# A layer of attention in which odd key runs swap their high and low parts, and the low-part score products of a piece's two halves run in rows 0 to 63 and 64 to 127 of the array

## What is computed

```python
qkv = x @ Wqkv + bqkv
...
scores = jnp.einsum('hnd,hmd->hnm', qh, kh) * SCALE
scores = scores + graph_bias * adj_matrix[None, :, :]
scores = jnp.where(attn_mask[None, :, :] == 0, jnp.float32(-1000000000.0), scores)
attn = jax.nn.softmax(scores, axis=-1)
out = jnp.einsum('hnm,hmd->hnd', attn, vh)
...
x = _layernorm(x + _L0_gnn_ref(x, adj, adj, L0_gnn_Wqkv, L0_gnn_bqkv, L0_gnn_Wout, L0_gnn_bout, L0_gnn_graph_bias), axis=-1)
x = _layernorm(x + _L1_gnn_ref(x, adj, L1_gnn_W, L1_gnn_a), axis=-1)
x = _layernorm(x + _L2_gnn_ref(x, adj, L2_gnn_W, L2_gnn_b), axis=-1)
x = _layernorm(x + _L3_gnn_ref(x, adj, L3_gnn_W), axis=-1)
```

## Time and profile before

| | |
|---|---|
| median of 3 runs | 2980.61 us (2979.36 to 2982.26) |
| the profiled execution's own time | 2979.79 us |
| its span | 2978.0 us, granted clock 0.997 |
| TensorE matmuls busy | 2938.3 us, 99% of the span |
| VectorE, ScalarE busy | 2090.7 us (70%), 1893.6 us (64%) |
| attention in its steady state | about 160 to 1557 us of the span |

### The profile page before, as it was taken

How to read it: one execution, slowest core, us unless ns; L and a number is a source line. 1 busy time by engine, 2 the same in 40 slices (tenths; PEclk the granted TensorE clock), 3 DMA queues, 4 the chain that set the end, 5 groups by cost and what they waited for, 6 DMA issues and landing times.

```text
span 2978.0 us, 45393 instructions
## 1 busy us (share of the span) xinstructions
PE 2938.3 (99%) x16612; PEld 2181.1 (73%) x16612; DVE 2090.7 (70%) x3587; ACT 1893.6 (64%) x2737; POOL 758.2 (25%) x458
## 2 busy tenths in 40 slices
PE   8999999999999999999999999999999999999998
PEld 6677777777777777777776555555568888788886
DVE  6777777777777777777756988888535555656554
ACT  4677777777777777777777777777644333533332
POOL 2123321233213332133303455444500101000000
PEclk9999999999999999999999999999999999999999
DMA  6555565565755657456527354454379898899882
GB/s 189 149 158 179 181 206 162 158 182 178 214 145 170 185 177 211 138 173 186 182 60 280 145 164 156 156 173 146 94 182 222 200 205 203 211 219 216 197 203 54
DMA packets 387181, 521.84 MB, mean 175 GB/s; under 512 B 38672, under 2 KB 316432, under 8 KB 370576
## 3 DMA queue, kind: packets, MB, share of 16 engines
q1 hardware_dynamic: 361920, 432.41, 52.5%
q10 hardware_dynamic: 18144, 66.07, 7.1%
q0 software_dynamic: 6896, 20.45, 2.4%
HBM read 430.71 MB, written 88.08 MB: 174 GB/s over the span
## 4 chain that ended last, share of the span: by engine, by line
PE 91%; DVE 3%; DMA 2%; issue 2%; ACT 1%; SPq 1%; POOLq 0%; POOL 0%; DVEq 0%; ACTq 0%
PE at_o L615 15%; PE gl_four L1507 14%; PE at_turn L589 11%; PE at_turn L602 9%; PE gl_quad L1560 7%; PE gl_quad L1562 7%; PE gl_quad L1561 7%; PE at_score L589 5%; PE at_score L602 5%; PE gl_quad L1490 4%; PE at_mixed L624 2%; PE gl_four L1533 2%; DMA adjT<-at_probs 1%; PE at_mixed L569 1%; DMA gl_early<-x 1%
## 5 line engine op out<-in xcount | busy, mean ns | idle before, releaser
L726 ACT ACTIVATE at_probs<-at_probs,at_minus_max 128x1024 f32<-128x1024 f32 x512 | 581.5, 1139 | 9.6 <-DVE at_minus_max L880 8.7
L875 DVE CUSTOM_DVE_ANT_0 at_probs<-at_turn,at_bias 128x1024 f32<-128x1024 f32 x336 | 407.9, 1214 | 184.5 <-PE at_turn L589 182.0
L512 POOL TENSOR_SCALAR at_masked<-at_bias 128x512 bf16<-128x512 f32 x180 | 365.3, 2050 | 495.3 <-DMA at_bias<-in_adj 403.1
L735 ACT ACTIVATE at_pT<-at_turn 128x1024 f32<-128x1024 f32 x342 | 345.7, 1023 | 219.5 <-PE at_turn L602 219.3
L615 PE MATMUL at_o<-at_pT,at_values 128*64 128x256 f32 x4096 | 470.3, 383 | 0.0
L1507 PE MATMUL gl_four<-gl_early,gl_first_wh 128*128 128x512 f32 x1024 | 462.4, 595 | 2.9 <-ACT gl_early L1634 2.9
L1659 ACT ACTIVATE gl_split<-gl_units 128x1024 fp32r<-128x1024 f32 x256 | 263.8, 1056 | 278.6 <-PE gl_quad L1562 278.6
L615 PEld LDWEIGHTS at_o<-at_pT,at_values 128*64 128x64 f32 x4096 | 282.9, 137 | 172.4 <-issue 43.1
L1560 PE MATMUL gl_quad<-gl_split,gl_rows_hi 128*128 128x512 f32 x1024 | 402.8, 393 | 4.3 <-DVE gl_split L1864 4.3
L1561 PE MATMUL gl_quad<-gl_split,gl_rows_hi 128*128 128x512 f32 x1024 | 398.9, 390 | 0.0
L1562 PE MATMUL gl_quad<-gl_split,gl_rows_lo 128*128 128x512 f32 x1024 | 398.9, 390 | 0.0
(11 more groups left out here) (136 smaller groups left out, 3853.1 us busy)
## 6 DMA issues: line engine op xcount, KB each, us to landing
gl_units<-adjT SPq DMA_DIRECT2D x512, 256.0 KB, 7.6
at_bias<-in_adj SPq DMA_DIRECT2D x128, 512.0 KB, 6.1
gl_first_weights<-in_adj SPq DMA_DIRECT2D x32, 2048.0 KB, 9.0
at_values<-v_heads ACTq DMA_DIRECT2D x126, 512.0 KB, 4.0
at_probs<-in_adj SPq DMA_DIRECT2D x208, 256.0 KB, 3.4
adjT<-at_probs SPq DMA_DIRECT2D x832, 64.0 KB, 2.6
gl_early<-x SPq DMA_DIRECT2D x160, 128.0 KB, 2.7
adjT<-gl_early SPq DMA_DIRECT2D x192, 64.0 KB, 1.8
```

The source lines that it names most:

```text
L512: pool.tensor_scalar(masked[:, g % MASKS, :], part, 0.0, MASKED / SCALE, ALU.is_equal, ALU.mult)\
L726: act.activation(part, part, ACT.Exp, bias=minus_max[:, k, t:t + 1], scale=1.0, accum_out=sums[:, k, t, pp:pp + 1]).then_inc(prob_ready, 1)
L735: act.activation(pT[:, j % PT_SLOTS, :], place[:], ACT.Copy).then_inc(pT_ready, 1)
L875: dve.tensor_tensor_reduce(out=ring[:, place_in_ring(u, pp), t, :], in0=place[:], in1=bias[:, t, at], scale=SCALE, scalar=LOWEST, op0=ALU. ...
```

## The change

Keys of odd runs are stored the other way round: high part in the half of the rows where even runs have the low one. For that `make_keys` computes a pair of an odd run as four matmuls of 64 columns, a head's keys landing in the other head's rows, and a second pair of bias columns (`bk[:, 1, :]`) is loaded by four small transfers on ScalarE's queue, ahead of its first instruction. `keep_keys` and `split_keys` swap their halves with the run's parity. The low part of the queries now stands in both halves of `q` part 1, for which `finish_q` gets one more instruction for each head; `clear_q` goes. `make_scores` first makes the part 0 products of both banks, and then part 1 of each bank over 64 rows only: where the first bank uses one half of the rows, the second uses the other, and so the two use different rows and different banks.

```diff
             def make_keys(u, pair):
...
+                bank = slice(pair * BANK, (pair + 1) * BANK)
                 for half in range(DH):
-                    last = pe.matmul(turn_bank[1][:, pair * BANK:(pair + 1) * BANK], wk[:, half, pair * P:(pair + 1) * P],
-                                     run_xT[:, u % 2, half * RUN:(half + 1) * RUN], start=half == 0, stop=half == DH - 1)
+                    of = run_xT[:, u % 2, half * RUN:(half + 1) * RUN]
+                    if u % 2 == 0:
+                        last = pe.matmul(turn_bank[1][:, bank], wk[:, half, pair * P:(pair + 1) * P], of,
+                                         start=half == 0, stop=half == DH - 1)
+                        continue
+                    for e in range(2):
+                        rows, others = halves(e)
+                        head = 2 * pair + e
+                        last = pe.matmul(turn_bank[1][others, bank], wk[:, half, head * HD:(head + 1) * HD], of,
+                                         start=half == 0, stop=half == DH - 1)
                 last.then_inc(key_made, 1)
...
             def make_scores(c, h, i, place=score_bank, unread=0, turned_out=0):
...
-                for bank in range(PIECE // BANK):
-                    at = slice(bank * BANK, (bank + 1) * BANK)
-                    col = pp * PIECE + bank * BANK
-                    for part in range(2):
-                        last = pe.matmul(place[:, at], q[:, q_place(h), part, t * P:(t + 1) * P],
-                                         kT[:, h, col:col + BANK], start=part == 0, stop=part == 1)
+                for part in range(2):
+                    for bank in range(PIECE // BANK):
+                        at = slice(bank * BANK, (bank + 1) * BANK)
+                        col = pp * PIECE + bank * BANK
+                        rows = halves((h + bank) % 2)[0] if part else slice(0, P)
+                        last = pe.matmul(place[:, at], q[rows, q_place(h), part, t * P:(t + 1) * P],
+                                         kT[rows, h, col:col + BANK], start=part == 0, stop=part == 1)
                 last.then_inc(score_made, 1)
...
         def scalar_program(act):
+            for pair in range(H // 2):
+                for e in range(2):
+                    rows, others = halves(e)
+                    at = D + (2 * pair + e) * HD
+                    act.dma_start(bk[others, 1, pair:pair + 1], bqkv[at:at + HD].rearrange("(e o) -> e o", o=1))\
+                       .then_inc(bias_rows_loaded, 16)
...
             def keep_keys(u, pair):
                 act.wait_ge(key_made, 2 * u + pair + 1)
                 for e in range(2):
-                    rows = slice(e * HD, (e + 1) * HD)
+                    rows, others = halves((e + u) % 2)
...
-                                   bias=bk[rows, pair:pair + 1]).then_inc(key_hi, 1)
+                                   bias=bk[rows, u % 2, pair:pair + 1]).then_inc(key_hi, 1)
...
-            def clear_q():
...
             def finish_q(c, h, e):
...
-                dve.scalar_tensor_tensor(out=q[rows, place, 1, :], in0=mixed_bank[rows, 0:CN], scalar=bias_row,
-                                         in1=q[rows, place, 0, :].bitcast(F32), op0=ALU.add, op1=ALU.subtract)
+                for half in (rows, others):
+                    dve.scalar_tensor_tensor(out=q[half, place, 1, :], in0=mixed_bank[rows, 0:CN], scalar=bias_row,
+                                             in1=q[rows, place, 0, :].bitcast(F32), op0=ALU.add, op1=ALU.subtract)
```

More of the change, by code:

```diff
@@ L257, in layer0_attention @@
         bv = in_first(7168, 2, D)
-        bk = first[:, 7680:7682]
+        bk = first[:, 7680:7684].rearrange("p (o a) -> p o a", o=2)
         v_out = pT[:, 0:2, :].rearrange("p k (t d) -> p k t d", t=RUN_TILES)
@@ L304, in layer0_attention @@
         WEIGHT_LOADS = 2
-        BIAS_ROW_LOADS = 4
+        BIAS_ROW_LOADS = 8
         CONST_LOADS = 6
@@ L421, in sync_program @@
             for pair in range(H // 2):
-                sync.dma_start(bk[:, pair:pair + 1], bqkv[D + pair * P:D + (pair + 1) * P].rearrange("(e o) -> e o", o=1))\
+                sync.dma_start(bk[:, 0, pair:pair + 1], bqkv[D + pair * P:D + (pair + 1) * P].rearrange("(e o) -> e o", o=1))\
                     .then_inc(bias_rows_loaded, 16)
@@ L796, in split_keys @@
                 for e in range(2):
-                    rows, others = slice(e * HD, (e + 1) * HD), slice((1 - e) * HD, (2 - e) * HD)
+                    rows, others = halves((e + u) % 2)
                     at = slice(u * RUN, (u + 1) * RUN)
@@ L800, in split_keys @@
                                              in0=turn_bank[1][rows, pair * BANK:(pair + 1) * BANK],
-                                             scalar=bk[rows, pair:pair + 1], in1=kT[rows, 2 * pair + e, at].bitcast(F32),
+                                             scalar=bk[rows, u % 2, pair:pair + 1], in1=kT[rows, 2 * pair + e, at].bitcast(F32),
                                              op0=ALU.add, op1=ALU.subtract).then_inc(key_lo, 1)
@@ L917, in add_step @@
                 last.then_inc(acc_ready, 1)
-            clear_q()
             dve.wait_ge(gain_loaded, 16)
```

## The result

The changed kernel takes 3043.93 us (median of 4 runs, 3040.11 to 3045.61) against 2979.99 us for the one before (4 runs, 2978.83 to 2982.26): the ratio is 1.0213, with a 95% interval of 1.0199 to 1.0228. It is slower by 64 us; the forecast was 3050 us and 70 us more.

The account below looks back on a forecast made before the run. The prediction took TensorE's stream to bound the kernel. Row halves at net +63.2 us, first pieces -1.5, keys +2.8 and VectorE's split +6 made +70.5 us, so 3050 us, with a range of 3025 to 3070.

Parts of the forecast that it names:

- TensorE's stream sets the time: In the attention, what TensorE's stream gains or loses per piece the kernel gains or loses, 512 times.
- The saving, 119 us: In each of 512 pieces, two part 1 products side by side save one matmul of 0.233 us: 119.3 us.
- The price of a change of shape, taken from column halves: Going between 128 rows and row halves on TensorE costs 0.202 us in, 0.155 or 0.202 out; 182.5 us together.
- Loads of a pair in series: Rival: the two weight loads of a 64-row pair run one behind the other, +54.8 us, 3105 us; 10 in 100.
- no overlap: Rival: a piece's two 64-row products run one behind the other, nothing saved, switches paid, 3170 us; 5 in 100.
- The row halves change for nothing: Rival: TensorE enters and leaves row halves without emptying, loads hidden, 119.3 us saved, about 2870 us; 14 in 100.
- half of the price: Rival: at TensorE's changes of shape only the pause or only the exposed loads are paid, 2963 or 2957 us; 14 in 100.
- VectorE's longer split, +6 us: 64 more `finish_q` instructions delay the reading that second transposes wait for, at 14 of 31 splits: +6 us, bounds 0 and 13.6.
- Keys, +2.8 us: At 8 places, four 64-column matmuls in pairs replace two full ones, adding a change in and out: 2.8 us.
- The first pieces, -1.5 us: About 12 first pieces fall where TensorE waits for others anyway: -1.5 us.
- The sum: All terms for the changed kernel together: 63.2 - 1.5 + 2.8 + 6 = +70.5 us, forecast 3050 us.

Follow-up runs that it names:

- the joined order: Changed kernel with a side's fourth piece and the next side's first made together ahead of the values, only their products in row halves: 2988.95 us, ratio 1.0036.

## Why the prediction was right

- *TensorE's stream sets the time.* Right: its clock and its busy share stayed, and every experiment that changed the stream moved the time by what the stream lost or gained.
- *The saving, 119 us.* Right: the pair has one start, and against two products in the same rows it is 115 to 121 us.
- *The price of a change of shape, taken from column halves.* This was the choice on which the sign hung, and the runs bear it out. Into row halves the pause is 0.33 - 0.233 = 0.10 us (0.095 forecast), the step to the transposes 0.43 (0.43), the first transpose 0.17 (0.16). The total of 182.5 us was measured nearly alone as 179 (172 in the execution with the clock of before). The Trainium skill's rule in "TensorEngine Tiling (Array Packing)", section Tiling Modes, that a change of mode drains TensorE, holds for row halves too. The trace agrees as far as it shows a pause of 0.10 us both into row halves and out of them. The Trainium skill's "TensorE: Matmul & The Clock Gate", Part 2, has row tiling take none of the additional buses; that does not make the change of shape cheaper, the pause is that of column halves.
- *Loads of a pair in series* (10 in 100) and *no overlap* (5 in 100): neither. A pair exposes one load of 0.107 us, and overlaps.
- *The row halves change for nothing,* and *half of the price:* refuted by the 172 to 179 us and by both steps in the timeline.
- *VectorE's longer split, +6 us.* The place and the mechanism were right, the size a little high: the waits rose from 6.3 to 9.9 us, 3.6 us, and before transposes they are 9 where some 14 were to appear (5 before the change). The prediction's count of such splits, 14 of 31, is one too high: in the trace of before 13 of the 31 have the reading 0.03 us behind them. The same term is 14 us where the pieces don't grow, just above the upper bound that was given (13.6). It is a term that depends on how late TensorE is, so it can't be added to other edits.
- *Keys, +2.8 us:* nothing is seen of it, the last matmul for keys starts at 80.1 us before and at 80.0 after. *The first pieces, -1.5 us:* wrong in sign, since the clock fell there, +3.5 us. These errors are small beside the 61 us of the steps; that they partly cancel is luck.
- *The sum.* The forecast's own, with the steps and the waits as measured, is 375 x 0.12 + 104 x (0.06 + 0.107) - 33 x 0.03 + 3.6 + 2.8 - 1.5 = 66 us; with 0 for the keys and 3.5 more for the clock it is 67, against 64 measured. The 33 pieces with values behind them gain 0.03 us each, since their way out was a change of shape already. The last 3 us aren't accounted for.

What stays open is why the clock falls around the first pieces when they use row halves, and whether the joined order would gain with VectorE's block turning placed elsewhere; neither was tried.

## What to carry to other kernels

Running two half-height products side by side saves one matmul, but going into and out of the half-height shape costs a fixed amount each time, here 0.20 us in and 0.155 to 0.20 us out, with the weight load that is exposed. Count the changes of shape per saved matmul before building the layout for it, and put such products beside work that has another shape already. Here one pair of 512-column products between full-height work didn't pay; one pair on either side of the column halves gained 0.05 us a side, and two pairs in a row ahead of them 0.25 us. An instruction added on an engine with a quarter of its time free can still cost a good part of its length (14 of 31 us here) if it stands ahead of the one reading that the bound engine waits for, and much more at a worse place (130 us), so look for what stands directly behind it.

## What the runs showed that I had not expected

In the stretches that I read no weight load went ahead across a change of shape, in either direction, for rows or for columns (the first step behind a change is 0.34 us for 512 columns), while inside one shape they did (0.23 us); a pair of loads for the two row halves costs what one does. And each of 29 stops of 2.6 us had some 3 us at a granted clock of 0.50 at its end, so that it cost some 1.8 us (53 / 29) more than its own length.
